# Two-stream cross-channel attention on one core: the turned loads, the first and the last steps put in another order

## The reference, cut to what matters

```
rgb = transpose(x); geo = transpose(ctx)                       # b, 1024, 128
attn = softmax(einsum('bhni,bhnj->bhij', q, k) * scale)        # 16 x 16 for each head
out  = einsum('bhnd,bhde->bhne', v, attn)
res_p2r = xca(rgb wq_rgb, geo wk_point, geo wv_point) @ proj_p2r.T
res_r2p = xca(geo wq_point, rgb wk_rgb, rgb wv_rgb) @ proj_r2p.T
result  = transpose(rgb + res_p2r) + transpose(geo + res_r2p)
```

## Time and profile before

| What | Value |
|---|---|
| Runs of the kernel before | 125.65, 125.70, 126.29 us, median 125.7 |
| The profiled execution's own time | 126.98 us |
| Its span, first to last instruction | 124.9 us |
| Busy share: PE, PEld, DVE, ACT, POOL | 94%, 85%, 59%, 67%, 62% |
| Chain that ended last | PE 79%, DMA 6%, issue 5%, ACT 4% |
| Moved | 36.35 MB, mean 291 GB/s |

### The profile page before, as it was taken

The page is one execution under the profiler, slowest core; times in us unless marked ns, Lnnn a source line. Parts: engine busy times, 40 slices in busy tenths (PEclk is TensorE's granted clock), DMA queues, the critical chain, the costliest instruction groups (busy, mean ns, idle before and its releaser), DMA issues.

```text
span 124.9 us, 2597 instructions
## 1 busy us (share of the span) xinstructions
PE 117.1 (94%) x826; PEld 106.1 (85%) x826; DVE 73.4 (59%) x214; ACT 84.2 (67%) x191; POOL 77.7 (62%) x41
## 2 busy tenths in 40 slices
PE   6869999999999999699999999999999999997991
PEld 6749898899898989598998989898989897985880
DVE  0035344725969595686259695959696965545210
ACT  4132869694878773886948777776877778588351
POOL 5000597877295955787772959593979595937700
PEclk9999999999999999999999999999999999999999
DMA  3999999999999999999999999999999997003435
GB/s 102 359 407 414 412 311 298 310 302 252 293 277 308 275 329 253 263 317 285 245 240 387 372 269 217 307 306 413 418 420 420 417 417 306 37 30 140 165 144 199
DMA packets 18669, 36.35 MB, mean 291 GB/s; under 512 B 1504, under 2 KB 12128, under 8 KB 18656
## 3 DMA queue, kind: packets, MB, share of 16 engines
q1 hardware_dynamic: 12928, 30.41, 73.9%
q10 hardware_dynamic: 5728, 5.77, 17.7%
HBM read 27.79 MB, written 8.39 MB: 290 GB/s over the span
## 4 chain that ended last, share of the span: by engine, by line
PE 79%; DMA 6%; issue 5%; ACT 4%; DVE 1%; ACTq 1%; SPq 1%
PE out_ps L316 33%; PE gram_bank L295 20%; DMA g_raw<-in_ctx_dram 6%; PE sy_bank L346 5%; PE gt_ps L274 3%; PE xt_ps L274 3%; PE t_bank L359 3%; PE sy_bank L370 3%; PE t_bank L360 3%; PE sy_bank L369 3%; ACT probs L456 2%; ACTq L158 1%; PE uv_bank L339 1%; PE uv_bank L337 1%; PE uv_bank L338 1%
## 5 line engine op out<-in xcount | busy, mean ns | idle before, releaser
L207 POOL TENSOR_TENSOR x_lo<-x_raw,x_hi 128x1024 fp32r<-128x1024 f32 x16 | 38.0, 2378 | 34.8 <-ACT x_hi L429 34.8
L210 POOL TENSOR_TENSOR g_lo<-g_raw,g_hi 128x1024 fp32r<-128x1024 f32 x16 | 38.1, 2382 | 4.3 <-ACT g_hi L429 4.2
L295 PE MATMUL gram_bank<-gt,xt 128*128 128x128 f32 x256 | 33.8, 275 | 0.0
L295 PEld LDWEIGHTS gram_bank<-gt,xt 128*128 128x128 f32 x256 | 31.2, 192 | 0.0
L436 ACT COPY out_sb<-out_ps 128x512 f32<-128x512 f32 x31 | 17.9, 582 | 5.7 <-PE out_ps L316 5.6
L429 ACT CAST g_hi<-g_raw 128x1024 fp32r<-128x1024 f32 x16 | 16.9, 1055 | 2.3 <-issue 2.2
L456 ACT ACTIVATE probs<-probs,min_neg 128x128 f32<-128x128 f32 x32 | 12.6, 395 | 7.8 <-DVE min_neg L553 7.8
L541 DVE COPY gt<-gt_ps 128x512 f32<-128x512 f32 x12 | 8.3, 689 | 15.2 <-PE gt_ps L274 15.2
L429 ACT CAST x_hi<-x_raw 128x1024 fp32r<-128x1024 f32 x16 | 16.6, 1037 | 0.6 <-DMA x_raw<-in_x_dram 0.6
L316 PE MATMUL out_ps<-x_hi,t_hi 128*128 128x512 f32 x31 | 13.6, 440 | 1.0 <-ACT t_hi L469 1.0
L534 DVE STREAM_TRANSPOSE gt<-gz 128x512 f32<-128x512 f32 x20 | 14.0, 702 | 0.0
(11 more groups left out here) (80 smaller groups left out, 205.2 us busy)
## 6 DMA issues: line engine op xcount, KB each, us to landing
x_raw<-in_x_dram SPq DMA_DIRECT2D x15, 512.0 KB, 14.6
g_raw<-in_ctx_dram SPq DMA_DIRECT2D x15, 512.0 KB, 15.2
out_dram<-out_sb SPq DMA_DIRECT2D x15, 512.0 KB, 14.6
xz<-in_x_dram SPq DMA_DIRECT2D x10, 256.0 KB, 13.4
gz<-in_ctx_dram SPq DMA_DIRECT2D x10, 256.0 KB, 14.1
xz<-in_x_dram ACTq DMA_DIRECT2D x10, 256.0 KB, 10.9
gz<-in_ctx_dram ACTq DMA_DIRECT2D x10, 256.0 KB, 14.1
x_raw<-in_x_dram SPq DMA_DIRECT2D x2, 256.0 KB, 4.4
```

The lines of the kernel that those rows point to most:

```text
L207: nc.gpsimd.tensor_tensor(x_lo[:, slot, :], x_raw[:, raw_slot, :], x_hi[:, slot, :].bitcast(F32), ALU.subtract).then_inc(x_lo_ready, 1)
L210: nc.gpsimd.tensor_tensor(g_lo[:, slot, :], g_raw[:, raw_slot, :], g_hi[:, slot, :].bitcast(F32), ALU.subtract).then_inc(g_lo_ready, 1)
L295: last = nc.tensor.matmul(gram_ps, xt[:, b % 2, cols], gt[:, b % 2, cols], start=(t == 0), stop=(t == TILES - 1))
```

## The change

SyncE now asks for a group at the head of the step, ahead of the plain loads of that step, and only after ScalarE has split x of batch i - 2 (`x_hi_ready` of i - 1). The groups go in steps 2, 4, 6, 8, 10, on SyncE and on ScalarE. TensorE's steps 0 and 1 are written out: the Gram halves of batch 0 now stand between the x turn and the ctx turn of batch 1. In TensorE's tail `y_product` of batch 15 comes after the first three products of batch 14, and `t_product` of 15 after the first six. In ScalarE's tail the exponents of batch 15 come ahead of the evacuation of batch 13's first half, and the evacuation of its second half ahead of the ctx split of batch 15.

```diff
-        first_steps = (2, 4, 6)
-        issued_in = {first_steps[group] if group < PAIRS else VECTOR_GROUPS[group - PAIRS][-1] + 1: group
-                     for group in range(len(VECTOR_GROUPS))}
+        issued_in = {step: group for group, step in enumerate((2, 4, 6, 8, 10))}
...
             for i in range(2, B):
+                group = issued_in.get(i)
+                if group is not None:
+
+                    sp.wait_ge(x_hi_ready, i - 1)
+                    if group >= PAIRS:
+                        pair_turned(sp, group - PAIRS)
+                    load_turned(sp, x_turn, xz, xz_loaded, group, (0, 1))
+                    load_turned(sp, g_turn, gz, gz_loaded, group, (0, 1))
                 for b in range(5, B):
                     if i == max(2, b - 1 if b in on_vector else b - 3):
                         if b >= RAW_SLOTS:
                             sp.wait_ge(x_lo_ready, b - RAW_SLOTS + 1)
                             sp.wait_ge(g_lo_ready, b - RAW_SLOTS + 1)
                         load_plain(b)
-                group = issued_in.get(i)
-                if group is not None:
-                    if group >= PAIRS:
-                        pair_turned(sp, group - PAIRS)
-                    load_turned(sp, x_turn, xz, xz_loaded, group, (0, 1))
-                    load_turned(sp, g_turn, gz, gz_loaded, group, (0, 1))
                 if i >= STORE_LAG:
                     store(i - STORE_LAG)
...
+            turn_half(0, 0)
+            turn_half(0, 1)
+            turn_x(1, 0)
+            gram_half(0, 0)
+            turn_g(1, 0)
+            turn_x(1, 1)
+            gram_half(0, 1)
+            turn_g(1, 1)
+
+            for i in range(2, B + 1):
...
             last_product(B - 3, 1)
+            last_product(B - 2, 0, 0, 3)
             y_product(B - 1)
-            last_product(B - 2, 0, 0, 3)
+            last_product(B - 2, 0, 3, 6)
             t_product(B - 1)
-            last_product(B - 2, 0, 3, 6)
             last_product(B - 2, 1)
...
             split_hi(B - 1, x_raw, x_loaded, x_hi, x_hi_ready)
+            exponents(B - 1)
             evacuate(B - 3, 0)
-            exponents(B - 1)
             t_high(B - 2)
+            evacuate(B - 3, 1)
             split_hi(B - 1, g_raw, g_loaded, g_hi, g_hi_ready)
-            evacuate(B - 3, 1)
             evacuate(B - 2, 0)
```

More of the change, by code:

```diff
@@ L276, in turn, with turn_x @@
                 last.then_inc(done, 1)
-            def turn_half(b, half):
+            def turn_x(b, half):
                 n = on_tensor.index(b)
@@ L283, in turn_half, with turn_g @@
                 turn(b, half, x_raw, x_first, x_loaded, xt_ps, xt_done)
+            def turn_g(b, half):
+                n = on_tensor.index(b)
                 if n or half:
@@ L286, in turn_half @@
                 turn(b, half, g_raw, g_first, g_loaded, gt_ps, gt_done)
+            def turn_half(b, half):
+                turn_x(b, half)
+                turn_g(b, half)
             def gram_half(b, half):
@@ L371, in s_product @@
                                  stop=True).then_inc(s_done, 1)
-            for i in range(B + 1):
+            turn_half(0, 0)
[7 more added lines that the diff above has]
+            for i in range(2, B + 1):
                 g, s, y, l = i - 1, i - 2, i - 3, i - 4
```

## The result

The changed kernel took 132.57 us (median of 4 runs, 131.04 to 133.23), the kernel before 126.0 us (median of 4, 125.65 to 128.67). The ratio is 1.0447, with a 95% interval of 1.0334 to 1.0561. The forecast was 123.9. A ratio counts only the runs within some 1.5% of the fastest of their kernel, so it also leaves out runs that late loads made long, while a median holds all runs; where the two differ both are given. The profiled execution of the changed kernel took 131.98 us with a span of 129.9, 5.0 us more than the one before.

The account below looks back on a forecast made before the run. The prediction took the chain of waits, nearly all TensorE, as the bound, with the DMA system second. Gains of 0.4 (head), 0.6 (middle) and 0.8 (tail), 1.8 us in sum, took the median from 125.7 to 123.9 us; range 123.0 to 125.2.

Parts of the forecast that it names:

- Head: TensorE's start: Gram half of batch 0 moved over the wait for ctx of batch 1, gain 0.4 us (ends 0 and 1.2).
- Tail: TensorE's end: y of batch 15 no longer waits, as its exponents start 0.85 us earlier; gain 0.8 us.
- the late g_lo: Tail: GpSimd's low part for batch 15 just fits at 118.7 us; 0.4 us late would make the gain 0.4.
- ScalarE's hold: Step 7: ScalarE's full request queue costs TensorE 1.2 us; later groups remove it, at most six requests open.
- the stall: Step 7: TensorE's 1.2 us loss, not sure in timed runs, so booked at 0.6 us for the median.
- SyncE's order and wait: Middle: later group requests, ahead of plain loads, cost 0; batch 9 in by 57 us, 2.5 us in time.
- lands near 80: Middle, from step 10 on: batch 11 lands near 80 us; its x was split at 86.35 before.
- rival 2: Step 9: plain batch 9 comes late if its flight passes 17 us; 127.5 to 130.5 us, chance 0.07.
- Rival 4: DMA queues run dry near 24 or 40 us from issuing late, all loads later; 124.4 us, chance 0.07.
- rival 1: Middle gives nothing, as timed runs lack the stall or it moves to step 8 or 10; 124.5 us, chance 0.3.
- The noise: Whole kernel: a measurement can tell some 0.5% (0.6 us) from no change.

## Why the prediction was wrong

**Head: right.** 0.4 us forecast, 0.40 measured. That it agrees so closely is luck: step 4 starts at 22.40 to 22.82 us in the sixteen profiled executions with the new head, and at 23.01 and 22.85 in the two with the old one, some 0.3 us apart in the mean. ScalarE's copy of uv started at 13.64 (13.65 forecast), the x turn behind it at 14.55, as forecast.

**Tail: right.** 0.8 forecast; from step 16 on 0.73 measured (0.6 to 0.8 over all traces), and no wait for the late g_lo.

**ScalarE's hold: right in its worth, but the hold did not go, and the gain was capped.** Step 7 gave the 1.2 us back. The prediction had the hold gone with at most six requests open; in step 8 the pair of gz requests still took 1.88 us, and step 8 lost 0.14. Its doubt whether other executions have the stall can be settled: all six profiled ones with group 3 in step 7 lost 0.5 to 2.8 us in that step, and none with group 3 in step 8 did. But the steps behind were not free to use the gain. With head and tails alone, x of batch 11 was split in the moment that it landed (0.8 us of waiting), as in the kernel before with 0.62 us. That row stood in the prediction: 1.6 us gained ahead of step 13 would have met a load that had no slack. I took it away with the sentence that batch 11 "lands near 80". It landed at 91.1.

**SyncE's order and wait: the step that failed.** The prediction had "Cost 0": 280 GB/s between 24 and 43 us, then group 2 at 250 and the plain batches 7 and 9 at 415, so batch 9 at 57 with 2.5 us in hand. It landed at 62.8, and step 9 lost 3.39 us. The term that was mis-sized is what the DMA engines have to move before batch 9 is in:

```profile
DMA packets 7288, 12.42 MB, mean 289 GB/s; under 512 B 554, under 2 KB 5117, under 8 KB 7284
...
DMA packets 3372, 5.78 MB, mean 292 GB/s; under 512 B 246, under 2 KB 2538, under 8 KB 3371
```

The first line is 0 to 43 us of the changed kernel, the second 43 to 62.8. By 43 us it had moved 12.4 MB, no less than the forecast's sum (5.8 + 2.1 + 4.2 = 12.1). After it the forecast counts 4.2 MB, and 5.8 were moved. Asked for in that time, and without a term in the sum, were batch 8 (44.84), the first store (47.83) and group 3 (ScalarE's half from 50.45, SyncE's from 51.95). At the measured 292 GB/s the 4.2 MB alone would have been in by 57.4, in time; the 5.8 MB at the 313 GB/s that the forecast's sum has for this stretch would have taken until 61.5, too late.

The rates were off too. They were 213 GB/s in 24 to 32 us and 194 in 40 to 48, not 280 and 250; I used the mean of a stretch of the old order, in which plain and group transfers were mixed, for a new order that parts them. At the old order's rates in those two stretches batch 9 would have been some 4.5 us earlier, an estimate from the 1.3 MB above, so a faster mix would have covered the missing term. Why the rate fell so low stays open. The flight of batch 9's ctx was 19.2 us, past the 17 us that rival 2 named as its point.

Rival 2 is what happened to batch 9; its 127.5 to 130.5 us at a chance of 0.07 were too low in both numbers, since it knew neither of batch 11 nor of the clock after the hole (3.8 us together). For batch 11 the failed step is the landing "near 80". How much of its lateness the change makes is not shown.

**The queues did not run dry.** Rival 4 is out: the DMA share in the two slow stretches is 1.01 and 1.11. The rule of the Trainium skill beside it (DMA: Bandwidth & Descriptors, Rules for kernel authors), to issue early, has the right sign here. But the version without the wait lost time as well (1.0247 and 1.0288), so late requests are not the whole of it.

**The noise.** The forecast's range assumed that runs differ by 0.6 us, as the three shown did. The kernel before took 125.4 to 133.3 us on one chip. The changed kernel's sixteen runs took 124.69 to 134.13: one near the 124.5 of rival 1, five from 126.8 to 129.5, ten from 131.0 on. Whether a load is missed differs from run to run, and what decides it was not found.

## What to carry to other kernels

A resource that is busy in every slice is a second bound, even where no engine waits for it: before a gain on the first bound is booked, look for the loads that land just as they are used, and cap the gain at their slack. When you work out by bytes when a load lands, count every transfer that is open in that time, on every queue. Bytes per us belong to a mix of transfers, not to a kernel; a new order needs the rate of its own mix, or a small DMA-only kernel that measures it. And when runs of one kernel scatter more than the effect, compare all runs of all versions on one chip: the changed kernel's ratio was 1.0447 in one measurement and 1.0099 in another.

## What the hardware showed that I had not expected

- Transfers of 1 KB rows into 32 partitions ran at 220 GB/s from one queue and at 303 from two. Plain loads of 4 KB rows ran at 388 and stores at 405.
- Two executions took 302.8 and 413.9 us, of versions whose other nine runs took 124.6 to 131.5. The trace of the first shows TensorE busy 99% of 300.7 us with a granted clock of 1.00, but a product of 512 columns took 820 ns where other traces have about 400; ScalarE's exponents took their usual 0.40 us. I have no explanation.
- The DMA rate differed between executions of the same program: in 40 to 48 us the changed kernel moved 194, 204 and 224 GB/s in three traces, and step 9, with batch 9, lost 3.4, 1.9 and 0.3 us. Its x of batch 11 was late in all three, by 3.4, 5.8 and 4.5 us, so that rate does not decide it. What sets either, other users of the memory among them, was not tried.
- TensorE's granted clock fell to half after waits of 1.21 and 0.51 us, with 0.26, 0.53 and 0.49 us of work in the three us from 92 to 95, and it stayed at full after waits of 1.56 and 1.43 us near 61.
